# First experts' results stored by slot and gathered back by token; attention in column pairs in batch order

## What is computed

```python
# layer 0, experts: the two best experts of each of 1536 rows
gates = zeros(T, 8).at[rows, topk_idx].add(topk_probs)
for e in range(8):
    h = gelu(flat_x @ w1[e] + b1[e])
    out = out + (h @ w2[e] + b2[e]) * gates[:, e:e + 1]
# layer 1, attention (12 heads of 16)
q_, k_ = relu(q) + SCALE, relu(k) + SCALE
kv = einsum('bnhe,bnhd->bhed', k_, v); k_sum = sum(k_, axis=1)
z = 1 / (einsum('bnhe,bhe->bnh', q_, k_sum) + EPS)
out = einsum('bnhe,bhed->bnhd', q_, kv) * z
out = out @ proj_w.T + proj_b
```

## Time and profile before

| | us |
|---|---|
| median of 3 runs | 462.23 |
| profiled execution, its own time | 462.79 |
| its span, first to last instruction | 461.0 |
| PE busy | 420.2 |
| DVE busy | 292.3 |
| POOL busy | 225.6 |
| ACT busy | 197.3 |
| mean granted clock of PE, share of full speed | 0.956 |

### The profile page before, as it was taken

One profiled execution on the slowest core, in us unless ns is written; L12 is line 12 of the kernel. 1 busy time (PEld: TensorE's weight loads), 2 busy tenths in 40 slices (PEclk: granted clock), 3 DMA queues, 4 the chain that ended last, 5 costly groups with the idle time before them and its releaser, 6 DMA issues.

```text
span 461.0 us, 10231 instructions
## 1 busy us (share of the span) xinstructions
PE 420.2 (91%) x3568; PEld 326.3 (71%) x3568; DVE 292.3 (63%) x1360; ACT 197.3 (43%) x374; POOL 225.6 (49%) x266
## 2 busy tenths in 40 slices
PE   7999998989788988989987988977999999999993
PEld 5653655637536877878844557933999999999993
DVE  6579999999782433333558336887465566556651
ACT  1287945441751111110123401546566566566660
POOL 4302798797035666666520000334456665665544
PEclk9799799999989999898979999998999999999998
DMA  8609400010132122222169999079233233333322
GB/s 233 96 1 227 113 0 3 1 35 1 58 102 70 60 61 70 69 70 70 47 195 236 224 225 217 15 137 139 50 62 50 54 62 63 51 55 61 51 25 27
DMA packets 40128, 39.02 MB, mean 85 GB/s; under 512 B 7575, under 2 KB 37259, under 8 KB 40079
## 3 DMA queue, kind: packets, MB, share of 16 engines
q1 hardware_dynamic: 28861, 23.05, 22.5%
q0 software_dynamic: 9312, 14.03, 15.3%
q10 hardware_dynamic: 1906, 1.30, 1.0%
HBM read 28.00 MB, written 11.06 MB: 85 GB/s over the span
## 4 chain that ended last, share of the span: by engine, by line
PE 66%; DVE 11%; DMA 10%; ACT 4%; POOL 4%; issue 4%; POOLq 1%; SPq 0%; DVEq 0%; another core or an unknown queue 0%; ACTq 0%
PE bank L1955 11%; PE bank L1990 10%; PE bank L1941 7%; PE bank L1983 7%; DMA out<-a,idx 5%; PE bank L2036 4%; POOL reg L707 3%; PE bank L1803 3%; PE bank L1964 2%; DMA xn<-expert_rows 2%; PE bank L1918 2%; ACT xn L834 2%; DMA reg<-xn_rows,idxs 1%; PE bank L2229 1%; DMA reg<-in_patchT 1%
## 5 line engine op out<-in xcount | busy, mean ns | idle before, releaser
L738 POOL DMA_INDIRECT reg<-xn_rows,idxs x62 | 60.5, 976 | 30.3 <-issue 16.6
L1955 PE MATMUL bank<-reg,xT 64*128 64x128 f32 x1116 | 72.6, 275 | 1.4 <-issue 1.1
L758 POOL DMA_INDIRECT out<-a,idx x31 | 50.3, 1622 | 46.7 <-DMA out<-a,idx 35.8
L1955 PEld LDWEIGHTS bank<-reg,xT 64*128 64x128 f32 x1116 | 68.6, 188 | 1.5 <-issue 1.0
L1990 PE MATMUL bank<-reg 64*128 64x192 f32 x744 | 69.0, 323 | 0.0
L1990 PEld LDWEIGHTS bank<-reg 64*128 64x128 f32 x744 | 63.4, 187 | 0.0
L1803 PE MATMUL bank<-con 128*128 128x512 bf16 x201 | 55.3, 435 | 0.0
L1045 ACT ACTIVATE reg<-reg 128x1152 f32 x31 | 36.1, 1163 | 30.8 <-PE bank L1990 30.8
L1574 DVE TENSOR_SCALAR a<-bank,gs 128x192 f32<-128x192 f32 x31 | 13.0, 418 | 53.2 <-PE bank L1990 53.2
L1024 ACT ACTIVATE reg<-bank 128x288 f32<-128x288 f32 x31 | 12.5, 410 | 77.4 <-PE bank L1941 62.9
L746 POOL DMA_INDIRECT expert_rows<-a,idx x31 | 30.6, 986 | 25.2 <-DVE a L1571 19.1
(11 more groups left out here) (363 smaller groups left out, 800.9 us busy)
## 6 DMA issues: line engine op xcount, KB each, us to landing
reg<-in_w2b SPq DMA_DIRECT2D x8, 576.0 KB, 10.2
reg<-in_w1b SPq DMA_DIRECT2D x8, 288.0 KB, 10.4
reg<-in_w1a SPq DMA_DIRECT2D x8, 216.0 KB
reg<-in_w2a SPq DMA_DIRECT2D x8, 216.0 KB
xn_rows<-xn SPq DMA_DIRECT2D x4, 384.0 KB, 2.7
reg<-in_w1b SPq DMA_DIRECT2D x8, 192.0 KB, 8.5
xn_rows<-xn SPq DMA_DIRECT2D x1, 1152.0 KB, 7.8
out<-h SPq DMA_DIRECT2D x1, 1152.0 KB
```

The source lines that it names most:

```text
L738: pool.indirect_dma_start(xs[:, i % RING, 0:(D, D2)[l]], None, xd[l], bass.IndirectOffsetOnAxis(ap=idxs[:, i:i + 1], axis=0)).then_inc(xs_ ...
L758: pool.indirect_dma_start(out, bass.IndirectOffsetOnAxis(ap=idx2[:, i:i + 1], axis=0), ys[:, i % YRING, :], None, compute_op=ALU.add).then ...
L1955: ins = MM(bank[2 + 2 * p + a][:, c * P:(c + 1) * P], w1r[rs, p, col:col + hc], xT64[rs, p, k, :], start=(c == 0 and k == 0), stop=(c == n ...
```

## The change

1. The 31 results of the first experts are stored by plain DMAs from SP's queue to `expert_rows`, slot by slot. POOL gathers only, while the tiles run. The addresses `idx2` of the first experts go.
2. When all stores have landed, POOL gathers both rows of each token back with 24 indirect DMAs (`results_back`): for each column the first choice into `xn` and the second into `a1`. They go in the order of the trios, a pair of columns per four gathers. SP issues the second experts' weights as soon as it has issued the last store.
3. `GROUPS[3]` becomes six pairs in the order of the trios, 0, 4 | 5, 1 | 6, 7 | 2, 8 | 9, 3 | 10, 11. DVE adds, PE transposes and multiplies pair by pair; keys and values of every pair use banks 2 and 3. `Q_PAIRS` makes queries of pairs 0 and 1, 2 and 3, 4, and 5.
4. Banks: queries and sums share 4 and 5, products of `numden` and of `out_proj` share 6 and 7 (the last round 2, 3 and 4, 5), transposes share 0 and 1.
5. PE runs 12 fillers more behind a wait for the fourth gather, and 4 fillers between the first keys and the second transposes.
6. The normalised rows for the second routing are stored in two parts, three rounds and then the last. The logits' preparation (`before_att`) goes in two halves.

```diff
-            def expert_dma(l):
...
-                    if l == 0:
-                        pool.indirect_dma_start(ybuf, bass.IndirectOffsetOnAxis(ap=idx2[:, i:i + 1], axis=0),
-                                                ys[:, i % YRING, :], None).then_inc(scat[i % YRING], 16)
-                        return
+            def first_dma():
+
+                rows_written(0)
+                for i in range(NT):
+                    gather(0, i)
+
+            def results_back(n):
+
+                for q in (2 * n, 2 * n + 1):
+                    for k, buf in enumerate((xn, a1)):
+                        a, g = k * NJ + ORDER[q], 2 * q + k
+                        if g >= YRING:
+                            pool.wait_ge(scat[g % YRING], 16 * (g // YRING))
+                        pool.indirect_dma_start(buf[:, q, :], None, ybuf,
+                                                bass.IndirectOffsetOnAxis(ap=sli[:, 0, a:a + 1], axis=0)
+                                                ).then_inc(scat[g % YRING], 16)
...
+            wait_results(pool, y_st)
+            results_back(0)
             link(nc.gpsimd.memset(vb[:, :, KC:KV], 1.0))
+            results_back(1)
             nc.gpsimd.memset(attT[KC:KC + 1, 1, :], 1.0).then_inc(att_ones, 1)
+            for n in range(2, NPAIR):
+                results_back(n)
```

SP's queue:

```diff
-            load_acc(sp, 0)
+            for i in range(NT):
+                sp.wait_ge(y_ev, i + 1)
+                sp.dma_start(ybuf[i * P:(i + 1) * P, :], ys[:, i % YRING, :]).then_inc(y_st[i % YRING], 16)
```

PE's waits around attention:

```diff
             keep_busy(18, 6)
-            t_pair(3, 0)
+            pe.wait_ge(scat[3], 16)
+            keep_busy(12, 6)
...
             def sums(i):
 
                 pe.wait_ge(att_ones, 1)
-                pe.wait_ge(k_ev, 2 * (1 + i // 2) + 2)
-                pe.wait_ge(v_ev, 2 * (1 + i // 2) + 2)
...
+                pairs = (3 * i + 2) // 2 + 1
+                pe.wait_ge(k_ev, pairs)
+                pe.wait_ge(v_ev, pairs)
+                pe.wait_ge(q_ev, 2 * i + 2)
```

PE's order, and DVE's, are written out anew:

```diff
+            rows_t(0, 0)
+            kv_mms(0)
+            keep_busy(4, 6)
+            rows_t(1, 0)
+            kv_mms(1)
+            q_mms(0)
+            rows_t(2, 0)
             sums(0)
             kv_mms(2)
             numden(0)
+            rows_t(3, 0)
+            kv_mms(3)
+            t_att(0)
+            q_mms(1)
             sums(1)
+            out_proj(0)
+            rows_t(4, 1)
+            kv_mms(4)
+            numden(1)
             q_mms(2)
-            t_att(0)
-            numden(1)
+            rows_t(5, 1)
+            t_att(1)
             sums(2)
-            out_proj(0)
-            t_att(1)
+            kv_mms(5)
+            out_proj(1)
+            q_mms(3)
             numden(2)
             sums(3)
-            out_proj(1)
             t_att(2)
             numden(3)
             out_proj(2)
```

More of the change, by code:

```diff
@@ L88 @@
 NCONST = NCON0 + 2 * P
-LANDED = [16 * (sum(1 for n in range(NT) if n % YRING == (i - 1) % YRING) + (i - 1) // YRING + 1) if i else 16
+LANDED = [16 * (SCAT0 + (i - 1) // YRING + 1) if i else 16
           for i in range(32)]
@@ L539, in turns, with wait_results @@
             return l * sum(1 for n in range(NT) if n % ring == i % ring) + i // ring
-        def wait_scatters(eng, l):
+        def wait_results(eng, done):
             for s in range(YRING):
[L543 to L552, removed]
+                eng.wait_ge(done[s], 16 * (sum(1 for i in range(NT) if i % YRING == s) + (0 if done is y_st else SCAT0)))
         @block.sync
@@ L1567, in evac_y @@
                     if i >= YRING:
[L1569 removed]
+                        dve.wait_ge((y_st, scat)[l][s], 16 * (turns(0, i, YRING) + l * SCAT0))
                     if l == 0:
@@ new lines, in kv_mms @@
+            def kv_mms(n):
+                pe.wait_ge(xT_ready, XT_BASE[3] + n + 1)
+                if n:
+                    pe.wait_ge(k_ev, n)
+                    pe.wait_ge(v_ev, n)
+                for a in range(2):
+                    MM(bank[2 + a][:, 0:WKV], xT3[:, n, 2 * a * P:(2 * a + 1) * P], qkvw[:, a, D:D + WKV],
+                       start=True, stop=False)
+                for a in range(2):
+                    rs = slice(64 * a, 64 * a + 64)
+                    ins = MM(bank[2 + a][:, 0:WKV], xT3[rs, n, P:2 * P], qkvw[rs, 2, D:D + WKV],
+                             start=False, stop=True)
+                ins.then_inc(kv_mm, 1)
@@ L2256, in half, with q_mms @@
+            def q_mms(c):
+                first, r = Q_PAIRS[c]
+                pairs = slice(first, first + r)
+                if c:
+                    pe.wait_ge(st_ev, c)
                 def half(m):
-                    return slice(m * 2 * P, (m + 1) * 2 * P)
+                    return slice(m * r * P, (m + 1) * r * P)
                 for m in range(2):
                     for a in range(2):
-                        MM(bank[6 + a][0:KC, half(m)], qkvw[:, a, m * KC:(m + 1) * KC],
-                           xT3[:, 2 * g:2 * g + 2, 2 * a * P:(2 * a + 1) * P], start=(m == 0), stop=False)
+                        MM(bank[4 + a][0:KC, half(m)], qkvw[:, a, m * KC:(m + 1) * KC],
+                           xT3[:, pairs, 2 * a * P:(2 * a + 1) * P], start=(m == 0), stop=False)
@@ L2265, in q_mms @@
                         rs = slice(64 * a, 64 * a + 64)
-                        ins = MM(bank[6 + a][0:KC, half(m)], qkvw[rs, 2, m * KC:(m + 1) * KC],
-                                 xT3[rs, 2 * g:2 * g + 2, P:2 * P], start=False, stop=(m == 1))
+                        ins = MM(bank[4 + a][0:KC, half(m)], qkvw[rs, 2, m * KC:(m + 1) * KC],
+                                 xT3[rs, pairs, P:2 * P], start=False, stop=(m == 1))
                 ins.then_inc(q_mm, 1)
```

359 lines of the change are left out of this document (171 added, 188 removed).

## The result

| | before | after |
|---|---|---|
| median of 4 runs, us | 460.46 (457.75 to 463.28) | 483.69 (482.06 to 487.08) |
| ratio after / before, 95% interval | | 1.051 (1.042 to 1.061) |
| profiled execution, its own time | 462.79 | 482.06 |
| its span | 461.0 | 480.0 |

The account below looks back on a forecast made before the run. PE was taken to bound first experts and attention. Start +3.8, work +1.2 and idle time +7.0 made +12.0 on 462.8; less 0.6 to the median, 474.2 us, 2.6% slower, range 464 to 480.

Parts of the forecast that it names:

- I take 0: First experts: moving scatters off POOL gains nothing, as PE never waits for them; 0 us, gain bounded by 10.1.
- Rival B: First experts speed up because POOL's 2.56 us per tile holds results back; -10.1 us, 464.1 us in all, chance 0.12.
- Start of attention, +3.8: PE's first transposes move from 242.0 to 245.8, set by the gathers' landing; +3.8 us.
- the 4.7 taken: Hand-over: time for the fourth gather to land, taken from token gathers during the start's loads; 4.7 us.
- the upper bound of 8.5: Hand-over: longest landing of the fourth gather, from the old loads back; 8.5 us, making the start 3.8 later.
- Work inside, +1.2: Attention: same products, plus four fillers (0.9 us) and some 0.3 for queries made apart; +1.2 us.
- Idle time, 13.3: Attention: PE's waits in the new order sum to 13.3 us against 6.3 today; +7.0 us.
- the second transposes: Attention: DVE and ACT work ahead of these runs past the four fillers, leaving PE idle; 1.2 us.
- the two longest gaps: Attention: PE waits ahead of sums(2), 2.6 us, and sums(3), 3.0 us, put down to DVE's query evacuation.
- Clock, none in the sum: PE: an idle gap may or may not cost 1.5 us through a lower clock; the sum includes none.
- Rival C: Attention: three gaps cost clock, 478.7 us, or gathers land late at 8.5 us, 478.0 us; chance 0.16.

Follow-up runs that it names:

- experiment 2: Changed kernel, with GpSimd issuing each first-experts gather twice, the second into columns nobody reads; one run, 513.2 us.
- experiment 8: Kernel before, with first experts' odd-tile results stored by SP to rows nobody reads instead of scattered; one run, 450.1 us.
- Experiment 3: Changed kernel, with SP issuing the second experts' weights only after all 24 gathers have landed; one run, 485.7 us.
- experiment 10: Changed kernel with result gathers in steps, queries evacuated first on VectorE, and SP's weights behind all 24 gathers; median 458.93 us, ratio 0.996 to before.
- Experiment 5: Changed kernel, with VectorE evacuating the queries of rounds 2 and 3 ahead of ln_end(4, 0), ratio(2) and before_att; median 476.24 us, ratio 1.030 to before.
- experiment 4: Kernel before, with results stored by slot and gathered back, 12 more fillers, but attention's old order and banks; median 476.12 us, ratio 1.032 to before.
- experiment 1: Changed kernel, with gathers of pairs 2 to 5 each waiting until TensorE transposed the pair two earlier; median 480.88 us, ratio 1.041 to before.
- experiment 6: Changed kernel with result gathers in steps, and SP's second-expert weights behind the first eight gathers; median 471.34 us, ratio 1.022 to before.
- experiment 7: Changed kernel with result gathers in steps, SP's weights behind the first eight gathers, and queries first on VectorE; median 463.08 us, ratio 1.002 to before.
- experiment 9: Changed kernel with result gathers in steps, queries first on VectorE, and SP's weights behind the first sixteen gathers; median 459.86 us, ratio 0.997 to before.
- experiment 11: Changed kernel with stepped result gathers, queries first, weights behind sixteen gathers, and first-experts gathers from tile 5 waiting for tile i - 5; 459.95 us, ratio 0.994.

## Why the prediction was wrong

**First experts, "I take 0".** This was the first step that failed. The reason given, that PE waits for no scatter, is true. What was missed is that ACT and DVE started late on products that PE had done, and that PE then waited for them. Rival B had the price (-10.1, measured -9.9) and the right engine, POOL's 2.56 us beside PE's 2.50, but the wrong link: not results held back behind POOL, but PE's signals held while POOL issues (experiments 2 and 8). The rows were there: "remote" ahead of ACT and DVE in the trace of before.

**Start of attention, +3.8; measured +7.4.** The first gather came 2.5 us after the last result (2.1 had been taken). From the fourth gather's issue (221.87) to the sum (229.83) it took 8.0 us, against the 4.7 taken; the upper bound of 8.5 was the nearer one. From the data to the transposes it took 4.3, as laid out. Experiment 3 shows the cause: with the weights held back, the whole from first gather to sum shrinks by 5 us. The prediction drew from the Trainium skill (DMA: Bandwidth & Descriptors, Queues, rings and completion order), where each DMA engine takes turns between the queues by packets, that such gathers would land in a few us. The trace agrees as far as both queues move packets side by side; but it was 8.0 us against 2.7 without the weights, more than that reading allowed for.

**Work inside, +1.2.** At full clock the products take 52.5 us (experiment 10) against 50.3: +2.1.

**Idle time, 13.3; measured 84.45 - 60.90 = 23.6.** Most of the gaps laid out came out close: 0.58 for transposes to keys, but for the first pair's, 1.58 (ACT took up transposes that ended at 234.65 only at 235.68); ahead of sums(0) 1.00 for 0.85, sums(1) 1.48 for 1.4, sums(2) 2.57 for 2.6, sums(3) 3.22 for 3.0, fourth transposes 1.07 for 1.4. One did not: the second transposes, 10.3 for 1.2, and that one is the hold, +9.1. Experiment 5 shows that the two longest gaps were set as told.

**Clock, none in the sum.** PE's busy time was 60.9 us against 52.5 at full clock, +8.4. Rival C had 4.5 for three gaps, and landing late as an alternative; the two came together, with the hold on top, which the range left out. The granted clock was 0.50 from 234.9 to 241.7, after PE had worked 0.55 of the 2.4 us ahead of it, and from 245.1 to 258.8, through the hole; then for 3.4 us behind each of the waits ahead of sums(2) and sums(3). Behind the hole PE worked 5.7 us at 0.50, so the hold cost its 9.1 us and, by an estimate from these rows, about 3 of the 8.4; the start's low clock cost about as much, each of the two waits 1.7.

So, on the forecast's +12.0: start +3.6, hold +9.1, clock +8.4, work +0.9, other gaps +1.2, together +35.2; less 9.9 in the first experts, 5.3 of chance at the start and 1.0 at the end: +19.0, the span's difference. That the difference missed by only 7.0 us (19.0 for 12.0) is luck: 16 us on the other side, 10 of them a gain that the sum put at nothing, hid most of the 23 us by which the start and attention were under-priced.

**What was right.** Slower, the first transposes held back by the gathers' landing, and the two longest gaps ahead of sums(2) and sums(3) behind the queries' evacuation. The range ended at 480, short of the median by 3.7 us: it left out both sides of C together (4.5 + 3.8 on top of 474.2 is 482.5), and the hold was in no rival.

## What to carry to other kernels

Where a consumer starts on its input long after the producer's row has ended, with both engines idle or running ahead, don't fill the gap with a reason from the code: look for "remote" in the waits, compare the end of each product with the start of what reads it, and look for an engine that issues transfers without a pause at that time. Plan the pauses of a queue of indirect transfers together with the signals that must pass beside it, and hold bulk loads back until the small transfers that start the next stage have landed. A gap of PE is priced with the clock behind it: here 23.6 us of idle time came with 8.4 us of slower products.

## What the hardware showed that was not expected

- Signals of PE to ACT, DVE and POOL came up to 11 us late while POOL issued indirect transfers 0.30 us apart; most of the long holds ended 1.1 to 1.6 us after POOL had ended its last transfer of the run (1.1 in the changed kernel), others about 3 us after (experiments 2 to 5); some shorter ones ended while the run still went on. Signals of DVE and ACT to each other passed in 0.03 to 0.4 us beside the same run of gathers (the changed kernel's first normalisation, at 232 to 234), where PE sent none; its next one, of the first transposes, was 1.0 us late. Whether a hold of 10 us takes other engines' signals too, no run shows.
- It takes more than a long run: in experiment 3 the keys of pair 0 and 1 passed in time, 15 and 21 us after POOL's first gather, and the next signals did not. In the first experts, behind their opening, it did not occur with one transfer per tile of 2.50 us, nor with three per two tiles; with two per tile it came back every few tiles. Counted in transfers 0.30 us apart: no signal was late where at most three came on end (the changed kernel and experiment 8, behind the opening), and many were where mostly four to eight did (before, experiment 2); yet in experiments 1, 6, 7, 9, 10 and 11 the 24 gathers, in fours with at least 0.5 us between, held none.
- What is held, the message or the product's completion itself, the profile can't tell, since ends of products are modelled. It was not tried apart.
- A gather of 128 rows landed and was summed 8.0 us after its issue beside the weights' loads and 2.7 us without them (experiment 3: issue at 226.69, sum at 229.41).
